# Value sums by thirds of a slab in one PSUM bank, and a ring of six PSUM banks numbered by a table

## The chip, the cores and the metric

One Trainium2 chip, one of its cores. The metric is the device time of one execution in microseconds (us). Engines are named PE (TensorE), DVE (VectorE), ACT (ScalarE), POOL (GpSimd) and SP (the queue that issues most transfers). The kernel is one launch of four blocks that run one after the other; all times below are of the whole launch.

## What is computed

The input is x, [4, 128, 96, 96]. The change touches only the second block, which works for this first half of the reference:

```python
kv = einsum('oc,bchw->bohw', qkv_w, gn(x))      # 1x1 convolution, 256 outputs
kv = dw3x3(kv, qkv_conv_w)                      # depthwise 3x3
k, v = split(kv, 2, axis=1)
q = ssl(gn(x), conv5_w, conv7_w, conv9_w)       # wavelet analysis, depthwise 3x3 per band, synthesis
# 8 heads of 16 channels: q and k normalised over the 9216 pixels
attn = softmax(einsum('bhdn,bhen->bhde', q, k) * temperature)
out = einsum('bhde,bhen->bhdn', attn, v)        # then a 1x1 projection, added to x
```

A second half (two binarised 3x3 convolutions with batch norm and a residual) follows; it is the fourth block.

## The kernel before

**The blocks.** `block_stats_and_projections` computes the group norm and the 1x1 projections and stores them (to about 190 us). `block_grams` (190 to 880 us) is the one the change touches. `block_attention` and `block_convolutions` follow.

**What `block_grams` does.** Its loop runs over NG = 32 slabs, numbered i = 0 to 31 here. One slab does two separate things. First, it handles 4 of the 128 channels, all four images, for keys and queries: separable filters as matrix products in split float16 (a high and a low part, three products for one), whose results go to `feat`; when four slabs (one head) are done, PE multiplies `feat` with itself into `gbank` (the gram) in pieces during the four slabs that follow. Second, it handles 12 rows of the values (SLAB = 12), all 128 channels: the depthwise 3x3 with nine taps. These value sums have nothing to do with the slab's filter jobs, but share the engines with them.

**Jobs.** A slab's filter work is 20 jobs, in the order of `SLOTS`, four rows of five: job 0 u, 1 kg, 2 mq, 3 s1, 4 tk; 5 kg, 6 s1, 7 mq, 8 u, 9 tk; 10 kg, 11 s1, 12 mq, 13 u, 14 tk; 15 kg, 16 s1, 17 mq, 18 u, 19 mq. Each job is summed by PE into one PSUM bank (L1059 to L1061 and L1069), then copied out as float16 by ACT (the high part, L965), then DVE subtracts that copy from the bank and so writes the low part (L1024). Here "low(n)" is the DVE step of job n. u and kg write `feat`, s1 writes `yh`/`yl`, mq writes `tmh`/`tml`, tk writes `tkh`/`tkl`. All three engines run the jobs in this order, with no reordering, and each waits by semaphores.

**What PE waits for.** Ahead of job n: that the bank is free, which is that low() of the bank's previous job is done (a ring of NB = 5 banks, so low(n-5)), and that its data are there. Job 0 (u) needs low(16) of the slab before, the s1 that wrote its operand; job 8 needs low(3), job 13 low(6), job 18 low(11). A DVE wait covers all earlier low() steps, since they run in order. After the last job of a row PE may run a piece of the gram of the head before (L1107, ten products).

**Value sums.** `seed` (L926, ACT) writes tap 0 of half a slab (6 rows of 96, 576 columns) into `vsum`, a PSUM tensor of two banks. `tap` (L1003, DVE) adds six more taps, each a scalar_tensor_tensor of 576 columns; the sixth writes to `vacc` in SBUF. Then the next half's seed may go. Each tap waits for the one before it. POOL adds taps 7 and 8 for the whole slab (`finish_slab`) after the last DVE tap. On DVE a tap runs right behind low(n) for each n in `TAP_AT`; on ACT a seed runs ahead of the copy of job n for each n in `SEED_AT`. `normalise` (four ACT instructions for the next slab's rows, L917) stands ahead of the copy of job 4, `high_x` ahead of that of job 13. In some slabs ACT also copies a finished gram (L944): ahead of job 11, right behind the copy of job 10, in the second slab that follows a head; right behind the copy of job 0 in the fourth.

**Kinds of slabs.** Slabs 0 to 3 have no gram beside them. From slab 4 on they repeat by four: kind 1 (i = 4, 8, ... 28) has gram pieces after jobs 9, 14 and 19; kind 2 after 4, 9 and 19, and the gram copy behind job 10; kind 3 after 4, 9, 14 and 19; kind 4 only a small product of edge terms after job 9, and the gram copy behind job 0. The slabs 4 to 27 are a hardware loop of three rounds of eight slabs; its two jumps back lie between slabs 11 and 12 and between 19 and 20. Slab 31 has no mq and tk jobs.

## Time and profile before

| | us |
|---|---|
| three timed runs | 1347.52, 1348.69, 1348.97 (median 1348.69) |
| the profiled execution, its own time | 1349.17 |
| its span, first to last instruction | 1347.2 |
| PE, DVE, ACT, POOL busy | 1158.6, 1009.5, 804.4, 533.7 |
| mean granted TensorE clock | 0.943 |

In the trace, DVE and ACT instructions overlap their neighbours: the next one starts some 0.08 us before the one ahead of it has ended. So what an instruction takes of its engine's time is the distance from its start to the next start, when nothing is waited for, and not its duration. A time in a "busy" column is a union of durations and hides short waits. PE's matmuls overlap in the same way.

### The profile page before, as it was taken

How to read it: one execution, taken by the hardware profiler on the slowest of the kernel's cores; microseconds unless marked ns; L12 is line 12 of the kernel's file. 1: busy time of each engine (PE TensorE's matmuls, PEld its weight loads, DVE VectorE, ACT ScalarE, POOL GpSimd, SP SyncE). 2: the span in 40 equal slices, each digit the busy share in tenths (PEclk: the TensorE clock that was granted, in tenths of full speed). 3: DMA queues.
4: the chain of work that ended last, by engine and by line, in shares of the span. 5: the costliest groups of instructions: out<-in, count | busy, mean ns of one | idle time of the engine just before them, and what ended most of it. 6: DMA issues, size and time to landing. Idle time of an engine off the chain costs nothing. (4 is left out here: it accounts for less than half of the span.)

```text
span 1347.2 us, 36311 instructions
## 1 busy us (share of the span) xinstructions
PE 1158.6 (86%) x12650; PEld 919.3 (68%) x12650; DVE 1009.5 (75%) x1802; ACT 804.4 (60%) x1414; POOL 533.7 (40%) x369
## 2 busy tenths in 40 slices
PE   0889978899999899998999999948999997999800
PEld 0445648889999899998999999825555554555500
DVE  6777557999999899998999999536767774153494
ACT  0567875777776677766777777212444446666292
POOL 6200023677686766867668776602000001000010
PEclk9999988999999899998999999878999998999955
DMA  9977793353553535535355354175778523000079
GB/s 320 417 245 304 304 301 78 94 150 101 126 151 98 131 103 129 147 102 133 98 133 145 101 138 114 41 264 196 265 244 279 190 82 123 1 0 0 1 312 406
DMA packets 148404, 221.24 MB, mean 164 GB/s; under 512 B 115202, under 2 KB 116492, under 8 KB 143896
## 3 DMA queue, kind: packets, MB, share of 16 engines
q1 hardware_dynamic: 136584, 152.18, 38.1%
q0 software_dynamic: 6480, 47.19, 9.2%
q10 hardware_dynamic: 5184, 19.76, 3.8%
q8 instruction: 101, 1.65, 0.6%
q14 instruction: 55, 0.45, 0.1%
HBM read 131.89 MB, written 87.20 MB: 163 GB/s over the span
## 5 line engine op out<-in xcount | busy, mean ns | idle before, releaser
L1746 PE MATMUL b_conv_bank<-b_sign,wsign 128*128 (+1 forms) x1728 | 299.9, 328 | 8.5 <-ACT b_sign L1544 7.5
L1017 DVE SCALAR_TENSOR_TENSOR b_value_sum<-b_vin,value_taps,b_value_sum 128x576 f32<-128x576 f32 x320 | 259.3, 810 | 16.3 <-ACT b_value_sum L934 15.5
L1746 PEld LDWEIGHTS b_conv_bank<-b_sign,wsign 128*128 128x128 bf16 x1728 | 168.1, 97 | 145.6 <-issue 31.7
L965 ACT CAST b_feat<-b_bank 96x400 f16<-96x400 f32 x255 | 125.7, 493 | 182.8 <-PE b_bank L1061 182.7
L1059 PE MATMUL b_bank<-b_tkh,b_kt 96*96 96x100 f16 x1536 | 224.3, 211 | 2.5 <-DVE b_tml L1040 2.2
L1060 PE MATMUL b_bank<-b_tkl,b_kt 96*96 96x100 f16 x1536 | 223.7, 211 | 0.0
L1061 PE MATMUL b_bank<-b_tkh,b_kt 96*96 96x100 f16 x1536 | 223.6, 211 | 0.0
L1059 PE MATMUL b_bank<-b_yh,b_tmh 96*96 96x200 f16 x768 | 195.1, 254 | 30.7 <-DVE b_feat L1024 14.4
L1059 PEld LDWEIGHTS b_bank<-b_tkh,b_kt 96*96 96x96 f16 x1536 | 195.2, 127 | 4.2 <-DVE b_tml L1040 2.5
L1061 PEld LDWEIGHTS b_bank<-b_tkh,b_kt 96*96 96x96 f16 x1536 | 195.3, 127 | 0.0
L1060 PEld LDWEIGHTS b_bank<-b_tkl,b_kt 96*96 96x96 f16 x1536 | 193.8, 126 | 0.0
L1061 PE MATMUL b_bank<-b_yh,b_tml 96*96 96x200 f16 x768 | 193.8, 252 | 0.0
L1060 PE MATMUL b_bank<-b_yl,b_tmh 96*96 96x200 f16 x768 | 193.6, 252 | 0.0
L812 POOL TENSOR_TENSOR b_vacc<-b_vacc,b_product 128x1152 f32<-128x1152 f32 x64 | 168.7, 2636 | 51.7 <-DVE b_vacc L1017 45.1
L1557 ACT CAST b_y<-b_conv_bank 128x384 f32 (+1 forms) x192 | 91.0, 475 | 126.5 <-PE b_conv_bank L1746 124.4
L1024 DVE TENSOR_TENSOR b_feat<-b_bank,b_feat 96x400 f16<-96x400 f32 x256 | 144.4, 564 | 25.9 <-ACT b_feat L965 21.1
L766 POOL TENSOR_TENSOR b_xl<-x_rows_store,b_xh 96x1536 f16<-96x1536 f32 x32 | 99.4, 3106 | 137.4 <-ACT b_xh L924 136.5
L1638 DVE BATCH_NORM_STATS2 b_bny<-b_y (+1 forms) x192 | 103.0, 553 | 58.3 <-ACT b_y L1557 57.8
L807 POOL TENSOR_TENSOR b_product<-b_vin,value_taps 128x1152 f32<-128x1152 f32 x64 | 134.8, 2106 | 6.0 <-POOL b_vacc L812 6.0
L1059 PEld LDWEIGHTS b_bank<-b_yh,b_tmh 96*96 96x96 f16 x768 | 95.1, 124 | 38.4 <-DVE b_feat L1024 18.6
L538 PE MATMUL b_pk<-b_x_first,b_w_image 128*128 128x384 f32 x288 | 102.2, 508 | 8.0 <-DVE b_khl L430 8.0
L965 ACT CAST b_tmh<-b_bank 96x504 f16<-96x504 f32 (+1 forms) x155 | 100.7, 650 | 0.0
(242 smaller groups left out, 2525.4 us busy)
## 6 DMA issues: line engine op xcount, KB each, us to landing
b_vin<-value_projection_scratch SPq DMA_DIRECT2D x32, 686.0 KB, 5.3
keys_scratch<-b_khl SPq DMA_DIRECT2D x24, 784.0 KB, 3.8
value_projection_scratch<-b_vout ACTq DMA_DIRECT2D x24, 784.0 KB, 4.7
b_kt<-keys_scratch SPq DMA_DIRECT2D x128, 147.0 KB, 3.3
x_rows_store<-in_x SPq DMA_DIRECT2D x128, 144.0 KB, 4.8
values_scratch<-b_vacc SPq DMA_DIRECT2D x32, 576.0 KB, 3.2
values<-values_scratch SPq DMA_DIRECT2D x48, 384.0 KB, 3.5
out<-xs SPq DMA_DIRECT2D x25, 576.0 KB, 6.9
```

Source lines behind the costliest of these rows:

```text
L538: nc.tensor.matmul(psum_k[g % NBK][:, 0:CH], w_image[:, b % 2, v, :], x[b][:, at:at + CH], start=True, stop=True).then_inc(s_mm, 1)
L766: nc.gpsimd.tensor_tensor(xh[1][:, slot, :, :, :].rearrange("h b c w -> h (b c w)"), xraw[:, slot, :], xh[0][:, slot, :, :, :].rearrange(" ...
L807: nc.gpsimd.tensor_tensor(vprod[:].rearrange("p (r c) -> p r c", c=W), vin[:, slot, :].rearrange("p (r c) -> p r c", c=WP)[:, t // 3:t // ...
L812: nc.gpsimd.tensor_tensor(vacc[:, slot, :], vacc[:, slot, :], vprod[:], ALU.add).then_inc(s_ptap, 1)
L965: nc.scalar.copy(*target(n, 0, k)).then_inc(s_hi, 1)
L1017: nc.vector.scalar_tensor_tensor(whole if t == DVE_TAPS[-1] else part, src, vtaps[:, t:t + 1], part, ALU.mult, ALU.add).then_inc(s_tap, 1)
L1024: nc.vector.tensor_tensor(out, src, high, ALU.subtract).then_inc(s_dve, 1)
L1059: nc.tensor.matmul(out, w_hi, m_hi, start=first, stop=False)
L1060: nc.tensor.matmul(out, w_hi, m_lo, start=False, stop=False)
L1061: return nc.tensor.matmul(out, w_lo, m_hi, start=False, stop=last)
L1638: V.bn_stats(bny[:, ds(r * RC + (b * NCH + k), 1), :].rearrange("p o s -> p (o s)"), y[:, b, ds(r * (RC * CH) + k * CH, CH)]).then_inc(s_b ...
L1746: ins = nc.tensor.matmul(cbank[k % NBK][:, 0:CH].rearrange("p (r c) -> p r c", c=W), p["wsign"][nth // NIMG][:, t * C:(t + 1) * C], padded ...
```

## The change

The value sums go by thirds of a slab in place of halves (PARTS = 3, PART = 4 rows, 384 columns), so `vsum` needs one PSUM bank in place of two. DVE issues 18 taps of 384 columns a slab in place of 12 of 576, ACT three seeds in place of two. The taps stand at new places, two of them behind low(4); the seeds stand ahead of jobs 1, 7 and 14 in place of 1 and 11. The bank that `vsum` gives up makes the ring of job banks six (NB = 6). Which job uses which bank is read from a table, `RING`: banks 0 and 1 are used every fifth job (0, 5, 10, 15 and 2, 7, 12, 17), the other four every sixth or seventh (1, 8, 14; 3, 9, 16; 4, 11, 18; 6, 13, 19). `last_use(n)` finds the job whose low() must be done. The eight builds ahead of the loop take their bank by their number modulo NB, as before. The rest is the same: the operations of the 20 jobs, their order, `NORMALISE`, `HIGH_X`, the gram pieces, POOL's work and all transfers.

```diff
@@ -576,12 +576,14 @@
         ana, map_place, map_diag, key_place, key_diag, null_cols = (
             p[n] for n in ("ana_parts", "map_place", "map_diag", "key_place", "key_diag", "null_cols"))
         PIECES = NIMG * H // STORE_ROWS // STORE_BUFS * 16
-        NB = 5
-        HALF = SLAB // 2
+        NB = 6
+        RING = (0, 2, 1, 3, 4, 0, 5, 1, 2, 3, 0, 4, 1, 5, 2, 0, 3, 1, 4, 5)
+        PARTS = 3
+        PART = SLAB // PARTS
         bank = [ctx.enter_context(nc.psum_tensor(f"b2_bank{i}", [C, 512], F32)) for i in range(NB)]
         gbank = ctx.enter_context(nc.psum_tensor("b2_gram", [C, 512], F32))
         last_gbank = [gbank, bank[0], bank[1]]
-        vsum = ctx.enter_context(nc.psum_tensor("b2_value_sum", [C, 2, 512], F32))
+        vsum = ctx.enter_context(nc.psum_tensor("b2_value_sum", [C, 512], F32))
 
         s_c = p["s_c"]
         s_z = sem("b2_pads_zeroed")
@@ -607,6 +609,11 @@
         s_gst = sem("b2_gram_stored")
         s_carry = sem("b2_wait_carrier")
 
+        def last_use(n):
+
+            return max(m for m in range(n) if RING[m] == RING[n]) if RING[n] in RING[:n] else max(
+                m for m in range(J) if RING[m] == RING[n]) - J
+
         NTK = -(-NKB // KPB)
         NTM = -(-NMB // MPB)
 
@@ -618,10 +625,10 @@
         )
         DVE_TAPS = (1, 2, 3, 4, 5, 6)
         POOL_TAPS = (7, 8)
-        NTAP = 2 * len(DVE_TAPS)
+        NTAP = PARTS * len(DVE_TAPS)
         PSTEPS = 2 * len(POOL_TAPS)
-        TAP_AT = (0, 2, 3, 5, 7, 8, 10, 12, 13, 15, 17, 18)
-        SEED_AT = (1, 11)
+        TAP_AT = (0, 1, 2, 3, 4, 4, 6, 7, 8, 9, 10, 11, 13, 14, 15, 16, 17, 18)
+        SEED_AT = (1, 7, 14)
         NORMALISE, HIGH_X = 4, 13
         LAG = {"s1": 0, "kg": 0, "u": 1}
         tk_jobs, mq_jobs = iter(range(NTK)), iter(range(NTM))
@@ -813,7 +820,7 @@
 
             def first_product(i, slot):
 
-                pool.wait_ge(s_seed, i * 2 + 1)
+                pool.wait_ge(s_seed, i * PARTS + 1)
                 pool.sem_inc(s_carry, 1)
                 product(slot, POOL_TAPS[0])
 
@@ -878,7 +885,7 @@
         def target(n, part, k):
 
             kind, c, old = jobs[n]
-            b = bank[n % NB]
+            b = bank[RING[n]]
             if kind == "s1":
                 return (ya[part][:, c % 2, :, 1:1 + SB], b[0:W, 0:NIMG * S2B].rearrange("p (n w) -> p n w", w=SB))
             if kind in builds:
@@ -923,16 +930,15 @@
                 act.wait_ge(s_xn, i + 1)
                 nc.scalar.copy(xh[0][:, slot, :, :, :].rearrange("h b c w -> h (b c w)"), xraw[:, slot, :]).then_inc(s_xh, 1)
 
-            def seed(k, i, half, loads):
+            def seed(k, i, part, loads):
 
                 slot = k % 2
-                if half == 0:
+                if part == 0:
                     act.wait_ge(s_vin[slot], loads * 16)
-                if half or not isinstance(i, int) or i:
-                    act.wait_ge(s_tap, i * NTAP + half * len(DVE_TAPS))
-                src = vin[:, slot, :].rearrange("p (r c) -> p r c", c=WP)[:, half * HALF:(half + 1) * HALF, 0:W]
-                nc.scalar.activation(vsum[:, :, 0:HALF // 2 * W].rearrange("p b (r c) -> p b r c", c=W),
-                                     src.rearrange("p (b r) c -> p b r c", b=2),
+                if part or not isinstance(i, int) or i:
+                    act.wait_ge(s_tap, i * NTAP + part * len(DVE_TAPS))
+                nc.scalar.activation(vsum[:, 0:PART * W].rearrange("p (r c) -> p r c", c=W),
+                                     vin[:, slot, :].rearrange("p (r c) -> p r c", c=WP)[:, part * PART:(part + 1) * PART, 0:W],
                                      ACT.Copy, scale=vtaps[:, 0:1]).then_inc(s_seed, 1)
 
             def copy_gram(head, e, gbank=gbank):
@@ -1002,19 +1008,18 @@
 
             def tap(k, i, m, loads):
 
-                slot, half, t = k % 2, m // len(DVE_TAPS), DVE_TAPS[m % len(DVE_TAPS)]
-                src = vin[:, slot, :].rearrange("p (r c) -> p r c", c=WP)[:, half * HALF + t // 3:(half + 1) * HALF + t // 3,
+                slot, part, t = k % 2, m // len(DVE_TAPS), DVE_TAPS[m % len(DVE_TAPS)]
+                src = vin[:, slot, :].rearrange("p (r c) -> p r c", c=WP)[:, part * PART + t // 3:(part + 1) * PART + t // 3,
                                                                           t % 3:t % 3 + W]
-                src = src.rearrange("p (b r) c -> p b r c", b=2)
-                whole = vacc[:, slot, half * HALF * W:(half + 1) * HALF * W].rearrange("p (b r c) -> p b r c", b=2, c=W)
-                part = vsum[:, :, 0:HALF // 2 * W].rearrange("p b (r c) -> p b r c", c=W)
+                done = vacc[:, slot, part * PART * W:(part + 1) * PART * W].rearrange("p (r c) -> p r c", c=W)
+                total = vsum[:, 0:PART * W].rearrange("p (r c) -> p r c", c=W)
                 if t == DVE_TAPS[0]:
-                    dve.wait_ge(s_seed, i * 2 + (half + 1))
+                    dve.wait_ge(s_seed, i * PARTS + (part + 1))
                 else:
                     dve.wait_ge(s_tap, i * NTAP + m)
                 if m == len(DVE_TAPS) - 1:
                     dve.wait_ge(s_vst[slot], loads * 16)
-                nc.vector.scalar_tensor_tensor(whole if t == DVE_TAPS[-1] else part, src, vtaps[:, t:t + 1], part,
+                nc.vector.scalar_tensor_tensor(done if t == DVE_TAPS[-1] else total, src, vtaps[:, t:t + 1], total,
                                                ALU.mult, ALU.add).then_inc(s_tap, 1)
 
             def low(n, k):
@@ -1029,7 +1034,7 @@
                     if active(n, how):
                         dve.wait_ge(s_hi, i * J + (count(n, how) + LEAD))
                         low(n, k)
-                    if n in TAP_AT:
+                    for _ in range(TAP_AT.count(n)):
                         tap(k, i, m, pairs + (k // 2 + 1))
                         m += 1
                 assert m == NTAP, m
@@ -1072,7 +1077,7 @@
 
             def run(n, k):
                 kind, c, old = jobs[n]
-                b = bank[n % NB]
+                b = bank[RING[n]]
                 slot = (k - old) % 2
                 ring = c % 2
                 if kind == "s1":
@@ -1136,9 +1141,9 @@
 
                 for n, (kind, c, old) in enumerate(jobs):
                     if active(n, how):
-                        m = n - NB if n >= NB else max(m for m in range(J) if m % NB == n % NB) - J
+                        m = last_use(n)
                         while m >= 0 and not active(m, how):
-                            m = m - NB if m >= NB else max(q for q in range(J) if q % NB == n % NB) - J
+                            m = last_use(m)
                         need(m)
                         if kind == "s1" and c == 0:
                             pe.wait_ge(s_xl, i + 1)
@@ -1153,7 +1158,7 @@
                         if kind in builds:
                             if c == 0:
                                 pe.wait_ge(s_rk if kind == "tk" else s_rm, i + 2)
-                            build(kind, c, bank[n % NB], (k + 1) % 2)
+                            build(kind, c, bank[RING[n]], (k + 1) % 2)
                         else:
                             run(n, k)
                     if gram is not None and n in row_end:
```

## Rows read from the trace of the kernel before

**Rows 1.** The page, span in 40 slices of 33.7 us, digits are tenths.

```profile
DVE  6777557999999899998999999536767774153494
PEclk9999988999999899998999999878999998999955
```

**Rows 2.** By slab: busy PE, PEld, DVE, ACT, POOL; clock, DMA share, GB/s.

```profile
261.80:281.40 19.60, 17.56 (x286) 16.64 (x286) 19.02 (x34) 14.24 (x29) 13.43 (x8) 1.00 0.52 119
531.50:551.10 19.60, 18.85 (x305) 18.43 (x306) 19.03 (x34) 14.09 (x27) 16.66 (x17) 1.00 0.36 104
551.10:572.20 21.10, 20.56 (x324) 20.01 (x323) 19.34 (x33) 15.43 (x29) 16.07 (x9) 1.00 0.65 147
572.20:592.10 19.90, 19.90 (x317) 19.45 (x316) 19.07 (x33) 14.10 (x27) 13.61 (x8) 1.00 0.46 117
592.10:612.90 20.80, 19.95 (x337) 19.00 (x335) 19.08 (x33) 15.32 (x30) 13.22 (x8) 1.00 0.54 138
612.90:638.30 25.40, 22.25 (x301) 22.04 (x302) 19.31 (x34) 14.20 (x27) 19.27 (x18) 0.80 0.35 97
```

**Rows 3.** Groups of instructions, 200 to 880 us: busy, mean ns, idle before, releasers.

```profile
L1059 PE MATMUL b_bank<-b_yh,b_tmh 96*96 96x200 f16 x768 | 195.1, 254 | 30.7 <-DVE b_feat L1024 14.4 <-DVE b_yl L1024 8.2 <-DVE b_tml L1024 4.1
```

**Rows 4.** Timeline of DVE, slab 3: start, duration, instruction, [idle before].

```profile
261.79 0.57 DVE L1024 TENSOR_TENSOR b_yl<-b_bank,b_yh 96x400 f16<-96x400 f32 x1
...
270.20 0.64 DVE L1024 TENSOR_TENSOR b_tkl<-b_bank,b_tkh 96x468 f16<-96x468 f32 x1 [0.58 <-ACT b_tkh L965]
...
276.01 0.81 DVE L1017 SCALAR_TENSOR_TENSOR b_value_sum<-b_vin,value_taps,b_value_sum 128x576 f32<-128x576 f32 x1
276.73 0.57 DVE L1024 TENSOR_TENSOR b_yl<-b_bank,b_yh 96x400 f16<-96x400 f32 x1
...
281.39 0.57 DVE L1024 TENSOR_TENSOR b_yl<-b_bank,b_yh 96x400 f16<-96x400 f32 x1
```

**Rows 5.** Timeline of PE at the start of slab 3.

```profile
262.50 0.26 PE L1059 MATMUL b_bank<-b_yh,b_tmh 96*96 96x200 f16 x1 [0.98 <-DVE b_yl L1024]
```

**Rows 6.** Timeline of ACT, slab 3, jobs 0 to 4.

```profile
264.97 0.74 ACT L934 ACTIVATE b_value_sum<-b_vin,value_taps 128x576 f32<-128x576 f32 x1 [0.20 <-DVE b_vacc L1017]
265.91 0.49 ACT L965 CAST b_feat<-b_bank 96x400 f16<-96x400 f32 x1 [0.20 <-PE b_bank L1061]
...
267.23 2.50 ACT L917 ACTIVATE x_rows_store<-x_rows_store,row_stats 96x384 f32<-96x384 f32 x4
269.63 0.54 ACT L965 CAST b_tkh<-b_bank 96x468 f16<-96x468 f32 x1
```

**Rows 7.** Timeline of DVE in the first block: 384 columns, and two dependent steps.

```profile
90.95 0.60 DVE L430 SCALAR_TENSOR_TENSOR b_khl<-b_pk,b_bias,b_khl 128x384 f16<-128x384 f32 x1
91.47 1.27 DVE L334 BATCH_NORM_STATS2 b_bn<-b_x_first 128x6 f32<-128x512 f32 x2
...
113.45 0.22 DVE L395 SCALAR_TENSOR_TENSOR b_col<-b_col 128x1 f32<-128x1 f32 x1
113.71 0.15 DVE L396 TENSOR_SCALAR b_col<-b_col 128x1 f32<-128x1 f32 x1
```

**Rows 8.** Timeline of DVE, kind 2 (551.1 to 572.2).

```profile
560.01 0.65 DVE L1024 TENSOR_TENSOR b_tkl<-b_bank,b_tkh 96x468 f16<-96x468 f32 x1 [0.59 <-ACT b_tkh L965]
...
566.68 0.82 DVE L1017 SCALAR_TENSOR_TENSOR b_value_sum<-b_vin,value_taps,b_value_sum 128x576 f32<-128x576 f32 x1 [0.79 <-ACT b_value_sum L934]
```

**Rows 9.** Timeline of ACT, kind 2, gram copy and second seed.

```profile
565.04 1.06 ACT L944 COPY b_gout<-b_gram 128x512 f32<-128x512 f32 x1
565.90 0.75 ACT L934 ACTIVATE b_value_sum<-b_vin,value_taps 128x576 f32<-128x576 f32 x1
```

**Rows 10.** Timeline of DVE, kind 4 (592.1 to 612.9).

```profile
597.59 0.82 DVE L1017 SCALAR_TENSOR_TENSOR b_value_sum<-b_vin,value_taps,b_value_sum 128x576 f32<-128x576 f32 x1 [0.95 <-ACT b_value_sum L934]
...
601.75 0.64 DVE L1024 TENSOR_TENSOR b_tkl<-b_bank,b_tkh 96x468 f16<-96x468 f32 x1 [0.35 <-ACT b_tkh L965]
```

**Rows 11.** Timeline of PE at the jump back ahead of slab 20.

```profile
616.05 0.39 PE L1059 MATMUL b_bank<-b_yh,b_tmh 96*96 96x200 f16 x1 [3.39 <-DVE b_feat L1024]
```

## The prediction

> **What bounds the kernel now.** The page's chain of work that ended last reaches back only to 916 us, behind the block in question, so it doesn't say what sets the pace there. The page's slices come first: in the slices of `block_grams` both PE and DVE stand at 9 tenths, and TensorE's clock is at its upper level but for three dips [rows 1]. So the table of busy time slab by slab is the view to read [rows 2]. It shows that the pace isn't one number. A slab without gram takes 19.6 us with PE busy 17.6 and DVE 19.0. In kind 3 PE is busy for all 19.9 us: there PE is the bound. Kind 2 takes 21.1 though DVE is busy 19.3, kind 4 takes 20.8. DVE does the same work in each slab, so its 19.0 says how near it stands to being the bound in all of them.
>
> Then the timeline of DVE in slab 3. From low(16) of the slab before (261.79) to the same step one slab on (281.39) are 19.60 us, with a single wait of note: 0.58 ahead of low(4) [rows 4]. I cut the slab there. The **front**, low(16) to low(4), is 270.20 - 261.79 = 8.41 us; the **rest**, low(4) to the next low(16), is 281.39 - 270.20 = 11.19 us, in which DVE never stands still: it is a sum of DVE's starts. The front is a chain over three engines: low(16) ends at 262.36, PE starts job 0 at 262.50 after an idle time that ended with it [rows 5], jobs 0 and 1 run, ACT copies job 1 at 265.91, then jobs 2 and 3, then `normalise` from 267.23, then job 4 at 269.63 [rows 6], and low(4) starts at 270.20 [rows 4].
>
> **What the change does to DVE's time.** A tap of 576 columns takes 276.73 - 276.01 = 0.72 us from start to next start [rows 4]. The trace has the same operation with PSUM input at 384 columns, in the first block: 91.47 - 90.95 = 0.52 us [rows 7]. Both fit 0.12 us plus a column each 1.04 ns, so the 0.12 is paid per instruction. Per slab the taps go from 12 x 0.72 = 8.64 us to 18 x 0.52 = 9.36 us. Two taps behind low(4) have nothing between them and the second waits for the first: start to start is then the duration plus about 0.04 us (0.22 and 0.26 in the two dependent steps, [rows 7]), 0.60 + 0.04 = 0.64 in place of 0.52, so 0.12 more. DVE's bill is 0.72 + 0.12 = 0.84 us a slab. The price of a tap is bounded below by 0.48 us (0.72 x 384 / 576, no price per instruction) and above by its duration of 0.60 us [rows 7]; I take 0.52, the row with the same operation, columns and kind of source.
>
> The Trainium skill, VectorE: DVE Perf Modes, section The TRN2 errata, speaks against the change: many small tiles pay a fixed latency each, so tile to 512 elements or more. By its formula for back-to-back fp32 work, (N + 151) / 0.96 ns, the smaller size costs 6 x 151 / 0.96 = 0.94 us a slab, an estimate, against the 0.72 that the rows give; the sum below would be some 7 us higher.
>
> **Where the new time lies.** In the front, DVE had 5 taps (behind 17, 18, 0, 2, 3) and gets 7 (16, 17, 18, 0 to 3): 5 x 0.72 = 3.60 against 7 x 0.52 = 3.64 us, and the 0.58 of idle time covers it. The chain there doesn't change: job 0 needs low(16) as data, which no bank changes, and `normalise` stays ahead of job 4. In the rest, 7 taps (behind 5, 7, 8, 10, 12, 13, 15) become 11: 7 x 0.72 = 5.04 against 11 x 0.52 + 0.12 = 5.84, so 11.19 becomes 11.99 us. Nothing covers that, if PE and ACT deliver in time.
>
> I walked the new order by these durations, low(16) at 0. low(4) 8.41, the two taps 8.97 and 9.61, low(5) 10.13. Seed 2 goes when the tap ends (10.2) and takes between 0.49 (two thirds of today's 0.74, [rows 6]) and 0.74 us; I take 0.59, near the middle, and even 0.74 has it done at 10.95, where the next tap wants it at 11.1. Job 10 (kg) needs low(5) in both kernels, bank 0 being used every fifth job; low(5) is now 1.1 us later, so PE idles until 10.75, but it still delivers job 10 to ACT at 12.6, and low(10) comes only at 14.8. Job 15 starts at 15.4 and is copied by 18.3, low(15) is due at 19.3. low(16) comes at 20.35. So DVE keeps full and **a slab without gram takes 20.4 us in place of 19.6**. I add 0.05 for the third hand-over of a seed.
>
> **What the sixth bank gives.** PE's waits for feat's low() ahead of u jobs (14.4 us, [rows 3]) are mostly those for the bank, at jobs 13 and 18; they go. But in a slab whose pace is DVE's, PE only waits at another job: job 10 and job 0. The gain is where PE was late. By kind, the same walk:
> - Kind 1 (19.54 before): front as before, rest +0.80, PE's gram pieces fall into its new gaps: **+0.86**.
> - Kind 2 (21.14: front 8.94, from 551.07 to 560.01 [rows 2, 8], and rest 12.20): the rest holds a stall of 0.79 [rows 8], because the gram copy of 1.06 us stands ahead of the second seed on ACT [rows 9], and some 0.2 behind it. The seeds now stand ahead of 7 and 14, neither behind the copy: 11.99. The front is long today because PE comes late to job 0, still at its gram piece; with DVE 0.8 later in kind 1, PE is less late and the front is 8.5. Sum 20.5: **-0.64**.
> - Kind 3 (19.93): PE-bound 19.9 [rows 2]; DVE now wants 20.4, above PE's sum: **+0.47**.
> - Kind 4 (20.80): its front of 9.61 has the gram copy and then the seed ahead of job 1, a stall of 0.95 on DVE [rows 10]. The copy stays there, the seed is 0.15 shorter and PE comes 0.3 earlier: 9.14. Rest +0.80: **+0.32**.
>
> **The sum.** Slabs 0 to 3: 4 x 0.85 = +3.4. Kind 1, seven: +6.0, less 0.4 at each of the two jumps back, where PE arrives that much earlier at a stall of 3.4 us [rows 11] that itself stays: -0.8. Kind 2, seven: -4.5. Kind 3, seven: +3.3. Kind 4 without slab 31, six: +1.9. Slab 31, all taps but fewer low() steps, so that six more pairs of taps are adjacent: its last low() 0.5 later: +0.5. Together +9.8 us on the profiled execution's own 1349.17 (which lies 0.5 above the median of 1348.69): **1359.0 us**. POOL, SP and transfers keep their order: the last DVE tap stays behind low(18). The block behind starts later by as much.
>
> **Rivals.**
> - *A tap's price goes by columns alone* (0.48 us, the lower bound). For it: the first operation at 384 columns writes float16 to SBUF, not PSUM, and today's tap spans two banks. Against it: the fixed 0.12 is the same at both sizes. Each slab is then 11 x 0.04 = 0.44 cheaper: 1359.0 - 32 x 0.44 = 1345 us, faster than before.
> - *Bubbles on PE are the bound and the sixth bank removes them.* All 14.4 us of bank waits go and DVE's bill hides: 1349.2 - 14.4 = 1335 us. Against it: DVE idles 0.58 us in slab 3 [rows 4], less than its bill. The Trainium skill, Trainium Kernel Development and Optimization, section Best Practices, says that consistent bubbles can mean that PSUM ran out; by that rule this case would be the outcome. The same bubbles are also what a ring looks like that waits for DVE.
> - *The bill hides and nothing is gained*: DVE's idle share in kinds 2 and 4 takes it, 1349 us. It needs every front to shorten, and only two can.
> - *Nothing comes back in kinds 2 to 4*: new waits behind seeds eat the gains, and all 32 slabs pay 0.8: 1349.2 + 26 = 1375 us. Speaks for it: low(7) has only 0.1 us to spare behind seed 2.
> - *The clock falls.* PE's idle now comes in two stretches of 1.5 us a slab (ahead of jobs 10 and 0). Waits of 1 us leave the clock at 2.4 GHz [rows 5, 2]; the one of 3.4 brings it to 1.2 GHz, mean 0.80 in that slab, and the slab takes 25.4 in place of 19.5 [rows 2, 11], of which 3.1 is the stall itself and 2.7 the slow clock. From a point between 1 and 3.4 us it decides; ten slabs (0 to 3 and some of kind 1) would give 1359 + 27 = 1386 us.
>
> **Chances.** Forecast 0.65 (1353 to 1366); columns alone 0.11; bubbles 0.04; hides 0.07; nothing comes back 0.08; the clock 0.05. What a measurement can tell from no change is about 0.2%, 2.7 us. Faster 0.15, same 0.09, slower 0.76. The range runs from 1347, which takes in half of the faster case's spread, to 1373: the error of 0.02 us in a tap's price alone is 18 x 0.02 x 25 DVE-bound slabs = 9 us.
>
> **What the profile after would show.** Right: 576 taps of 384 columns, 0.52 us from start to start and 0.64 for the pair behind low(4); slabs of 20.4 without gram; DVE without a wait from low(4) to low(16) in all kinds; ACT's normalise still ahead of DVE's one idle stretch; PE's idle time ahead of job 10 on feat's low(5). Wrong: taps of 0.48; waits of DVE on seeds; slabs of 19.6; more stretches at 1.2 GHz.

## The result and the profile after

| | before | after |
|---|---|---|
| median of 8 runs each, us | 1348.24 (1346.06 to 1352.02) | 1354.55 (1352.98 to 1358.85) |
| the profiled execution, its own time and span | 1349.17, 1347.2 | 1354.76, 1353.1 |
| DVE, ACT busy, us | 1009.5, 804.4 | 1028.0, 815.0 |
| mean granted TensorE clock | 0.943 | 0.945 |

The changed kernel is slower: ratio 1.0055, 95% interval 1.0039 to 1.007. The forecast was 1359.0.

The page of after, the slices that answer to [rows 1], and two of its costliest groups (instruction, count, busy us, mean ns, idle time before it and what ended that):

```profile
DVE  6767557999999899998999999636767764153494
...
PEclk9999988999999899999999999877999998999955
...
L1022 DVE SCALAR_TENSOR_TENSOR b_value_sum<-b_vin,value_taps,b_value_sum 128x384 f32<-128x384 f32 x480 | 294.4, 613 | 8.7 <-ACT b_value_sum L940 8.5
L1064 PE MATMUL b_bank<-b_yh,b_tmh 96*96 96x200 f16 x768 | 195.0, 254 | 24.3 <-DVE b_yl L1029 10.7
```

The taps are at 384 columns (480 here, and 96 that write `vacc`), and PE's idle time ahead of u jobs fell from 30.7 us [rows 3] to 24.3. Ahead of the kg jobs it rose from 0.2 to 14.5, all of it a wait for DVE. From 200 to 880 us, before and then after:

```profile
L1059 PE MATMUL b_bank<-b_tkh,b_kt 96*96 96x100 f16 x1525 | 221.5, 211 | 0.2
L1064 PE MATMUL b_bank<-b_tkh,b_kt 96*96 96x100 f16 x1524 | 221.0, 211 | 14.5 <-DVE b_feat L1029 14.5
```

So PE stands still in these two groups for 38.8 us in place of 30.9, with one bank more.

The windows by slab, from low(16) to low(16), answer to [rows 2]: slab 3, then slabs 16 to 20, which are kinds 1, 2, 3, 4 and the slab behind the second jump back (slab 20, itself of kind 1). Columns as there (length, busy PE, PEld, DVE, ACT, POOL, granted clock, DMA share, GB/s).

```profile
263.55:283.91 20.36, 17.25 (x286) 16.63 (x286) 19.77 (x39) 14.64 (x29) 13.44 (x8) 1.00 0.50 130
535.09:555.49 20.40, 19.36 (x309) 18.72 (x310) 19.71 (x40) 14.24 (x28) 15.82 (x17) 1.00 0.37 107
555.49:575.96 20.47, 20.47 (x323) 19.97 (x321) 19.75 (x39) 15.84 (x31) 15.74 (x9) 1.00 0.56 144
575.96:596.36 20.40, 20.27 (x320) 19.65 (x319) 19.71 (x40) 14.14 (x27) 14.28 (x8) 1.00 0.47 124
596.36:617.29 20.93, 19.38 (x332) 18.53 (x329) 19.75 (x39) 16.09 (x32) 13.77 (x8) 1.00 0.52 133
617.29:640.97 23.68, 20.94 (x309) 20.32 (x310) 19.86 (x40) 14.13 (x28) 19.07 (x18) 0.93 0.40 111
```

The slabs have become nearly equal, 20.4 us, with DVE busy 19.7 of them; kind 4 keeps half a microsecond above that. The last row is the surprise: 25.4 before, 23.68 now.

The timeline of DVE in slab 3, against [rows 4] (start, duration, instruction, idle time before it):

```profile
263.55 0.58 DVE L1029 TENSOR_TENSOR b_yl<-b_bank,b_yh 96x400 f16<-96x400 f32 x1
...
271.98 0.64 DVE L1029 TENSOR_TENSOR b_tkl<-b_bank,b_tkh 96x468 f16<-96x468 f32 x1 [0.56 <-ACT b_tkh L971]
272.54 0.61 DVE L1022 SCALAR_TENSOR_TENSOR b_value_sum<-b_vin,value_taps,b_value_sum 128x384 f32<-128x384 f32 x1
273.18 0.62 DVE L1022 SCALAR_TENSOR_TENSOR b_vacc<-b_vin,value_taps,b_value_sum 128x384 f32<-128x384 f32 x1
273.71 0.56 DVE L1029 TENSOR_TENSOR b_feat<-b_bank,b_feat 96x400 f16<-96x400 f32 x1
...
278.88 0.61 DVE L1022 SCALAR_TENSOR_TENSOR b_value_sum<-b_vin,value_taps,b_value_sum 128x384 f32<-128x384 f32 x1
279.39 0.57 DVE L1029 TENSOR_TENSOR b_yl<-b_bank,b_yh 96x400 f16<-96x400 f32 x1
...
283.91 0.58 DVE L1029 TENSOR_TENSOR b_yl<-b_bank,b_yh 96x400 f16<-96x400 f32 x1
```

A tap takes 279.39 - 278.88 = 0.51 to 0.52 us from start to start, the first of the adjacent pair 273.18 - 272.54 = 0.64. The front is 8.43 us (8.41 before), with the same idle time ahead of low(4); the rest is 11.93 (11.19 before) without a wait.

PE in the same slab, its two waits of over 1 us:

```profile
264.28 0.26 PE L1064 MATMUL b_bank<-b_yh,b_tmh 96*96 96x200 f16 x1 [1.31 <-DVE b_yl L1029]
274.33 0.24 PE L1064 MATMUL b_bank<-b_tkh,b_kt 96*96 96x100 f16 x1 [1.41 <-DVE b_feat L1029]
```

They stand ahead of job 0 and of job 10, as forecast. The waits for the bank at jobs 13 and 18 (0.41 and 0.47 us in slab 3 before) have gone, and PE now waits that much and more at these two places, with 0.38 ahead of job 15.

### The profile page after: what moved, and what is told of

Its sections match the earlier page's. It is cut to its first block and busy times, and to the rows that moved or that the text cites. A ratio compares the mean times of both kernels' runs of the same rounds, so it can differ in the third digit from the quotient of the medians.

```text
span 1353.1 us, 36508 instructions
## 1 busy us (share of the span) xinstructions
PE 1158.7 (86%) x12650; PEld 918.0 (68%) x12650; DVE 1028.0 (76%) x1994; ACT 815.0 (60%) x1446; POOL 533.8 (39%) x369
## 5 line engine op out<-in xcount | busy, mean ns | idle before, releaser
L1022 DVE SCALAR_TENSOR_TENSOR b_value_sum<-b_vin,value_taps,b_value_sum 128x384 f32<-128x384 f32 x480 | 294.4, 613 | 8.7 <-ACT b_value_sum L940 8.5
L1064 PE MATMUL b_bank<-b_tkh,b_kt 96*96 96x100 f16 x1536 | 224.1, 211 | 17.2 <-DVE b_feat L1029 14.5
L1064 PE MATMUL b_bank<-b_yh,b_tmh 96*96 96x200 f16 x768 | 195.0, 254 | 24.3 <-DVE b_yl L1029 10.7
L1064 PEld LDWEIGHTS b_bank<-b_tkh,b_kt 96*96 96x96 f16 x1536 | 194.4, 127 | 23.8 <-DVE b_feat L1029 19.5
L1029 DVE TENSOR_TENSOR b_tml<-b_bank,b_tmh 96x504 f16<-96x504 f32 (+1 forms) x155 | 100.4, 648 | 0.0
```

What stands on the lines that cost most here:

```text
L1022: nc.vector.scalar_tensor_tensor(done if t == DVE_TAPS[-1] else total, src, vtaps[:, t:t + 1], total, ALU.mult, ALU.add).then_inc(s_tap, 1)
L1029: nc.vector.tensor_tensor(out, src, high, ALU.subtract).then_inc(s_dve, 1)
L1064: nc.tensor.matmul(out, w_hi, m_hi, start=first, stop=False)
```

## The experiments

Times are medians; each ratio is against the kernel before on the same chip, with its 95% interval. Slab times are read from low(16) to low(16) as above.

**How far the slabs repeat.** A second profile of each of the two kernels (1348.54 and 1354.79 us) gives slabs 1 to 31 within 0.03 us of the first, but for the two behind a jump back and slab 21 of the kernel before (21.44 us, again 21.54). Behind the jumps, before takes 25.42 and 25.35 us, again 24.96 and 25.53; after 24.96 and 23.68, again 23.84 and 24.98. Differences of 0.1 us in a kind can be read from one profile, a single jump can't; the two jumps together differ between the kernels by 2.1 us in the first pair of profiles and by 1.7 in the second.

**Is it the thirds, and what is the sixth bank worth?** `e1_thirds_five_banks` keeps the thirds and gives the bank back:

```diff
-        NB = 6
-        RING = (0, 2, 1, 3, 4, 0, 5, 1, 2, 3, 0, 4, 1, 5, 2, 0, 3, 1, 4, 5)
+        NB = 5
+        RING = (0, 1, 2, 3, 4) * 4
```

> The changed kernel with the ring back at five banks, every bank used each fifth job; thirds, taps and seeds stay. My theory: slabs without gram run at DVE's sum from low(4) to low(16), the banks set only where PE waits, and what kinds 2 to 4 gained came from the seeds' new places and from DVE being later, not from the bank. Then slabs stay at 20.35, 20.4, 20.5, 20.4 and 20.9 us and the time within 1.5 us of the changed kernel's 1354.6. Rival, the sixth bank pays: kind 2 goes back to 21.1 and kind 4 up by 0.3, some 6 us in all, 1360.

Measured: 1357.6 us, ratio 1.0066 (1.0048 to 1.0083). All kinds are within 0.03 us of after but for kind 2, 20.69 instead of 20.47. So the thirds, with their new places for taps and seeds, carry the whole loss and most of the gain in kind 2, and the sixth bank is worth 0.2 us in each of seven slabs, 1.5 us. The ratios, each against the kernel before timed beside it, say the same: 1.0066 against 1.0055, 1.5 us. The medians of e1 and after are 3.0 us apart; the kernel before was itself 1.1 us slower beside e1, and the two slabs behind a jump (25.50 and 24.13 us), which vary by as much, took 1.0 more. What the bank is worth in the kernels with thirds below, where PE waits elsewhere, wasn't run.

**Does moving a tap, with no work added or taken away, take the loss back?** `e2_pair_in_front` moves one of the two taps from behind low(4) to behind low(3), from the rest into the front:

```diff
-        TAP_AT = (0, 1, 2, 3, 4, 4, 6, 7, 8, 9, 10, 11, 13, 14, 15, 16, 17, 18)
+        TAP_AT = (0, 1, 2, 3, 3, 4, 6, 7, 8, 9, 10, 11, 13, 14, 15, 16, 17, 18)
```

> The changed kernel with one of the two taps behind low(4) moved behind low(3), so that the pair that waits for itself stands there and eight taps lie in the front, ten in the rest. My theory: the front's idle time of 0.56 us covers the moved tap (front 8.4 to 8.5), the rest loses 0.64 us and goes to 11.3. Slab without gram 19.8 in place of 20.35; kind 1 19.8, kind 2 20.0, kind 3 20.4 (PE-bound), kind 4 20.4: 13 us less than the changed kernel, 1341 to 1343, under the kernel before. Rival: PE or the chain over ACT bounds, the place of a tap is worth nothing, 1354.

Measured: 1340.42 us, ratio 0.9934 (0.9911 to 0.9957). Slabs without gram 19.72, kinds 1 to 4 19.65, 20.37, 19.73, 21.09. DVE and windows of this kernel, slab 3, and the slab behind the first jump:

```profile
272.45 1.27 DVE L1022 SCALAR_TENSOR_TENSOR b_value_sum<-b_vin,value_taps,b_value_sum 128x384 f32<-128x384 f32 x2
273.62 0.64 DVE L1029 TENSOR_TENSOR b_tkl<-b_bank,b_tkh 96x468 f16<-96x468 f32 x1
```

```profile
265.20:284.92 19.72, 17.25 (x286) 16.64 (x286) 19.68 (x40) 14.62 (x29) 13.44 (x8) 1.00 0.53 127
446.60:468.67 22.07, 19.60 (x308) 18.86 (x309) 19.68 (x40) 14.09 (x28) 17.51 (x17) 1.00 0.43 120
```

The idle time ahead of low(4) is filled by the pair. DVE's sum, 19.72 us, is now the length of a slab without gram; that is the floor of the thirds as they are ordered. Moved work was worth more than the removed waits of PE. The total is in part luck. The expectation was 20.0, 20.4 and 20.4 us for kinds 2, 3 and 4, and only the misses' opposite signs bring the sum near it: in kind 4 a feat copy and a seed still make DVE wait 0.50 and 0.79 us, and the tap that was moved has nothing to fill. And by the profiles 3.4 us of the gain on after lie at the jumps, where the clock did not fall at all in e2 (see below); the other slabs from 1 to 30 give 11.4.

**Did ACT's `normalise` set the front?** `e5_normalise_at_5` moves it behind the copy of job 4, `e4_normalise_at_9` ahead of the copy of job 9:

```diff
-        NORMALISE, HIGH_X = 4, 13
+        NORMALISE, HIGH_X = 5, 13
```

> The changed kernel with ACT's four normalise instructions ahead of the copy of job 5, so behind that of job 4 and ahead of the second seed. In the run with them at job 9 the front fell to DVE's own sum (7.77 us), but they then stood behind the seed that waits for the sixth tap, and the copy of job 9 came 0.88 us late. At 5 they end 1.3 us before that seed is due. My theory: front 7.8, rest 11.95, slab without gram 19.75, kind 1 19.8, kind 2 20.1, kind 3 20.3 (PE), kind 4 20.5: 1341 to 1343. Rival: the normalise only moves its price from one wait to the next, 1352 or more.

> The changed kernel with ACT's four normalise instructions ahead of the copy of job 9 in place of job 4. My theory: they are what low(4) waits for at the end of the front; without them DVE runs from low(16) to low(4) at its own sum, 7.8 to 7.9 us in place of 8.4. Slab without gram 19.9, kind 1 19.9, kind 2 20.0, kind 3 20.4 (PE-bound), kind 4 20.5: 11 to 12 us less than the changed kernel, about 1343. Rival: the front is set by job 0 waiting for low(16), then 1354.

Measured: at 5 1342.9 us, ratio 0.9944 (0.9923 to 0.9965); at 9 1365.3, ratio 1.0123 (1.0107 to 1.014). ACT and DVE with `normalise` at 5:

```profile
266.25 0.58 ACT L971 CAST b_tkh<-b_bank 96x468 f16<-96x468 f32 x1
266.70 2.51 ACT L924 ACTIVATE x_rows_store<-x_rows_store,row_stats 96x384 f32<-96x384 f32 x4
```

```profile
260.82 0.57 DVE L1029 TENSOR_TENSOR b_yl<-b_bank,b_yh 96x400 f16<-96x400 f32 x1
...
268.60 0.64 DVE L1029 TENSOR_TENSOR b_tkl<-b_bank,b_tkh 96x468 f16<-96x468 f32 x1
```

The front is 7.78 us, all of it DVE's own work, and the slab 19.72: the 2.5 us of `normalise` ahead of job 4 did set it. Kind 4 stayed at 21.07 us where 20.5 had been expected, for the same two waits as in e2 (0.48 and 0.79). The two slabs behind a jump took 24.74 and 24.46 us, and each of the slabs behind them, 13 and 21, 21.24 in place of the 20.27 of its kind, PE being busy throughout. With `normalise` at 9 the front is as short (7.77), and the gain is lost further on:

```profile
273.30 0.58 ACT L940 ACTIVATE b_value_sum<-b_vin,value_taps 128x384 f32<-128x384 f32 x1 [1.87 <-DVE b_vacc L1022]
273.82 0.67 ACT L971 CAST b_tmh<-b_bank 96x504 f16<-96x504 f32 x1
274.37 0.48 ACT L971 CAST b_feat<-b_bank 96x400 f16<-96x400 f32 x1
274.75 2.51 ACT L924 ACTIVATE x_rows_store<-x_rows_store,row_stats 96x384 f32<-96x384 f32 x4
277.15 0.57 ACT L971 CAST b_tkh<-b_bank 96x468 f16<-96x468 f32 x1
```

ACT has 1.87 us of nothing to do, but it spends them in the wait of the second seed for the sixth tap, ahead of `normalise`. Copy 9 comes late, low(9) waits 0.88 us for it, and the slab takes 20.68:

```profile
277.75 0.64 DVE L1029 TENSOR_TENSOR b_tkl<-b_bank,b_tkh 96x468 f16<-96x468 f32 x1 [0.88 <-ACT b_tkh L971]
```

I had taken ACT's idle time as free at any place of its queue; in an engine that works in order it is free only where the idle time itself stands.

**Is kind 2's gain a gain of the thirds?** `e3_copies_moved` is the kernel before with only ACT's gram copies at other places, so that no seed stands right behind one:

```diff
-        START, COPY_AT, NULL_AT = [0, 6], [5, 11, 14], 12
+        START, COPY_AT, NULL_AT = [0, 6], [(1, 15), (3, 5), (3, 15)], 12
...
-                    if gram is not None and n - 1 in [-1] + row_end and chunk(k, n) in COPY_AT:
-                        copy_gram(gram, COPY_AT.index(chunk(k, n)))
+                    if gram is not None and (k % GPH, n) in COPY_AT:
+                        copy_gram(gram, COPY_AT.index((k % GPH, n)))
```

> The kernel before with ACT's gram copies moved: the first from behind job 10 to behind job 15 of kind 2, the second from behind job 0 to behind job 5 of kind 4. Halves, five banks, taps and seeds as before. My theory: the stalls of 0.79 and 0.95 us ahead of a tap go; kind 2 comes from 21.1 to about 20.2, kind 3 stays PE-bound and takes part of it back, kind 4 loses 0.3: about 1 us a head, 1340 to 1342 against 1348.2. It shows that kind 2's gain in the changed kernel is no merit of thirds or banks. Rival: PE bounds these slabs, nothing moves, 1348.

Measured: 1340.94 us, ratio 0.993 (0.9908 to 0.9952), kinds 1 to 4 at 19.54, 20.29, 20.05, 20.52.

```profile
301.06:321.35 20.29, 20.29 (x323) 19.94 (x322) 19.32 (x33) 15.33 (x29) 16.18 (x9) 1.00 0.44 113
```

Kind 2 is at PE's own sum (busy 20.29 of 20.29) with halves and five banks. So the better order of seed and gram copy, which needs neither thirds nor a bank, gives more in kind 2 (21.13 to 20.29) than the whole change does (to 20.48). In the changed kernel 0.2 of the 0.65 us is the sixth bank, by e1; that the rest is this order fits the wait of 0.79 us that has gone [rows 8, 9], and wasn't run by itself with thirds.

**Do the two cures add up?** `e7_pair_front_and_copies` is the changed kernel with the edits of e2 and e3. `e6_halves_split_normalise` is e3 with `normalise` cut up, images 0 and 1 ahead of job 4, image 2 ahead of 5, image 3 ahead of 6. `e8_halves_copy_behind_8` is e6 with the second gram copy behind job 8 instead of 5, that is (3, 8) for (3, 5).

```diff
-        NORMALISE, HIGH_X = 4, 13
+        NORMALISE, HIGH_X = {4: (0, 1), 5: (2,), 6: (3,)}, 13
```

> The changed kernel (thirds, six banks) with both cheap moves: one of the paired taps from behind low(4) to behind low(3), and the gram copies behind job 15 of kind 2 and job 5 of kind 4. My theory: kind 4, 21.1 us in the run with the pair alone because of the copy and the seed ahead of job 1, comes to 19.8 to 20.1; slab without gram stays 19.7, kind 1 19.7, kind 2 20.0, kind 3 20.3: 79.9 a head against 80.8, so 6 us under that run, 1334 to 1336. Rival: kind 4 only pays what kind 3's late PE leaves, 1340.

> The kernel before (halves, five banks, twelve taps) with the gram copies moved as in the run of that change, and normalise in pieces: two images ahead of the copy of job 4, one ahead of 5, one ahead of 6. My theory: DVE's twelve large taps are the cheaper bill (18.97 us a slab against 19.7), and with nothing late on ACT the slabs come to 19.05 without gram, 19.2, 19.9, 20.6, 19.5 by kind: some 14 us under the kernel before, 1334, under every variant with thirds. Rival: with five banks PE waits for banks as soon as DVE is full, no better than the run with the copies alone, 1341.

> The kernel before with halves, five banks, normalise in pieces as in the run with split normalise, and the second gram copy behind job 8 of kind 4 in place of 5. My theory: the 0.45 us that low(6) waited in kind 4 goes, 20.5 becomes 20.0 there: 3 us less, 1337.5. Rival: the copy's 0.85 us lands on the copy of job 9 or on the seed ahead of 11, no change, 1340.8.

Measured: e7 1340.6 us, ratio 0.9952 (0.9936 to 0.9968); e6 1340.81, ratio 0.9927 (0.9903 to 0.9951); e8 1351.84, ratio 1.0018 (0.9999 to 1.0037). None of them passes e2 and e3, and all three theories missed; e7 and e6 came out at their rivals' times. In e7 kind 2 fell to 19.96, as hoped, kind 3 took 19.90, and kind 4 stayed at 21.05, where 19.8 to 20.1 had been expected: 80.5 us a head in place of 79.9:

```profile
585.52:606.57 21.05, 19.97 (x339) 19.18 (x337) 19.95 (x40) 16.23 (x33) 14.08 (x8) 1.00 0.53 137
```

Kinds 2 and 3 are now PE's (busy 19.96 of 19.96, and 19.90 of 19.90), and in kind 4 DVE waits 0.50 and 0.52 us for feat copies; that PE enters kind 4 late, as the rival had it, fits this and wasn't tested apart. In e6 slabs without gram fell to 18.93 us and kind 1 to 18.87, but kinds 2 and 3 are PE's (busy for all of 20.66 and 20.05) and kind 4 stayed at 20.48. Kind 2 took back 0.37 of the 0.67 us that kind 1 gave: what one kind gives, the next takes, as PE's work is not spread evenly over them. One of its slabs shows more:

```profile
241.39:260.32 18.93, 17.16 (x286) 16.62 (x286) 18.93 (x34) 14.24 (x28) 13.46 (x8) 1.00 0.43 116
260.32:282.16 21.84, 20.35 (x286) 19.81 (x286) 19.22 (x34) 14.30 (x28) 13.41 (x8) 0.84 0.51 127
```

The same work twice, and in the second slab the clock is at its lower level (1.2 GHz) for 6.8 us from 261.0 on, though PE's longest wait around it is 0.98 us and in the first of the two rows, with the clock up throughout, PE did the same. It happened once in this execution, cost that slab 2.9 us, and its trigger stays open. In e8 the product of edge terms (L1122) waits for the gram copy, which now lies behind the copies of jobs 7 and 8; PE and the window of that slab:

```profile
520.33 0.96 PE L1122 MATMUL b_gram<-b_edge 96*16 96x16 f32 x32 [1.84 <-ACT b_gout L946]
```

```profile
508.35:532.10 23.75, 21.91 (x331) 21.59 (x329) 19.46 (x34) 15.27 (x29) 14.10 (x8) 0.86 0.40 107
```

1.84 us of waiting, and the clock falls at 521.3 for 6.8 us. Four slabs on, the same wait (1.85 us) leaves it up:

```profile
591.67:613.11 21.44, 19.44 (x337) 18.94 (x334) 19.38 (x33) 15.34 (x30) 13.20 (x8) 1.00 0.47 123
```

All six slabs of kind 4 with a whole job list have this wait, 1.84 to 1.86 us. In three of them the clock falls for 6.8 us and the slab takes 23.3 to 23.8, in one for 3.4 (22.18), in two not at all (21.44), against 20.48 in e6. So the copy costs 1 us a slab by the wait and up to 2.3 more by the clock. I had priced the copy by DVE's and ACT's queues and not by its reader on PE.

**The jumps back.** They were the largest miss of the prediction, so the last two runs take them away: `e9_halves_unrolled` is the kernel before, `e10_thirds_unrolled` the changed one, each with the 24 looped slabs written out.

```diff
-            with pe.Fori(0, LOOPS) as hh:
+            for hh in range(LOOPS):
```

and the same on SP, POOL, ACT and DVE, the rest unchanged.

> The kernel before with the 24 slabs of its hardware loop written out (no jump back on any engine), all else the same. Theory (the two slabs behind a jump take 25.4 us in place of 19.5 only because of the jump: PE's wait of 3.4 to 4.1 us and the slow clock that follows it): slabs 12 and 20 take 19.55 us like every kind 1, the clock stays at its upper level from 228 us to the end of the block, and the time falls by 5.87 + 5.80 = 11.7 us (less 0.3 more in slab 21), to 1349 - 12 = 1337 us (1335 to 1339). Rival (the wait is the fetch of instructions as such, and code that is written out pays it elsewhere, a little in every slab): slabs 12 and 20 come down but others rise, 1343 to 1350 us, with more idle time of the engines that nothing of the kernel releases.

> The changed kernel with its 24 looped slabs written out, all else the same. Theory (by the slabs the change costs some 10 us, and 2 to 3 of them came back at the two jumps only because PE's wait there is shorter and the clock falls for less time): slabs 12 and 20 take 20.4 us like every kind 1, the time falls by only 4.55 + 3.27 = 7.8 us, to 1354.6 - 7.8 = 1347 us (1345 to 1349), so 9 to 10 us above the kernel before with the same loop written out, where the two kernels with loops differ by 6. The end of the block still has the clock at its lower level for some 10 us, 3 longer than in the kernel before. Rival (the gain at the jumps is one of execution to execution, and the two kernels differ by the same 6 us without jumps): 1343 us.

Measured: e9 1340.37 us, ratio 0.9928 (0.9909 to 0.9947); e10 1346.01, ratio 0.9982 (0.9964 to 1.0). PE at job 0 of slab 12, where the jump was, in before, after, e9 and e10, one fence each:

```profile
448.05 0.40 PE L1059 MATMUL b_bank<-b_yh,b_tmh 96*96 96x200 f16 x1 [4.09 <-DVE b_tml L1024]
```

```profile
450.81 0.40 PE L1064 MATMUL b_bank<-b_yh,b_tmh 96*96 96x200 f16 x1 [3.07 <-DVE b_tml L1029]
```

```profile
442.56 0.26 PE L1059 MATMUL b_bank<-b_yh,b_tmh 96*96 96x200 f16 x1 [0.98 <-DVE b_yl L1024]
```

```profile
447.78 0.26 PE L1064 MATMUL b_bank<-b_yh,b_tmh 96*96 96x200 f16 x1 [1.31 <-DVE b_yl L1029]
```

And the windows of slab 12 in e9, then e10:

```profile
441.85:461.46 19.61, 18.80 (x305) 18.41 (x306) 19.03 (x34) 14.07 (x27) 16.93 (x17) 1.00 0.41 115
```

```profile
447.07:467.44 20.37, 19.34 (x309) 18.74 (x310) 19.78 (x40) 14.25 (x28) 16.02 (x17) 1.00 0.41 115
```

Without the jump both kernels start job 0 0.71 us after low(16), the clock stays at 2.4 GHz through the whole stretch from 226 to 848 us, and slabs 12 and 20 cost what every kind 1 costs. So the 5.4 to 6.0 us that a jump costs the kernel before are the jump's alone. The DVE step that the two rows with a jump name as the releaser isn't what job 0 needs: that is low(16), which ended 3.25 us ahead of it in the kernel before.

The DMA records of the traces show what arrives in between. The page of the profile lists a queue q8 of kind instruction; its loads are of 16 KiB. In all 24 jumps of the twelve profiles with a loop, the last of these loads ahead of job 0 starts 2.6 to 3.4 us ahead of it: with halves from 0.04 us ahead of low(16) to 0.93 behind it, with thirds from 1.10 us ahead of it to level with it. In e9 and e10 none starts in the 5 us ahead of job 0 of these slabs. The Trainium skill, Runtime: NRT & Kernel Launch, section Instruction fetch mechanics, says that a taken branch breaks the sequential fetch of instructions, and that one whose target isn't at hand stalls until the target has been fetched. The trace agrees, with these loads and with waits of 2.34 to 4.09 us; that job 0 waits for the load is argued from the times, as no view names it as the releaser.

From low(16) of slab 0 to low(16) of slab 30 the two kernels with loops differ by 629.86 - 626.40 = 3.5 us, the two without by 621.91 - 614.75 = 7.2. So the change costs its slabs 7.2 us, and 3.7 of that came back at the jumps, somewhat more than the theory's 2 to 3. The totals didn't follow it. e10 is within its range, but e9, expected at 1335 to 1339, lies between its theory and its rival, so that the two differ by 1346.0 - 1340.4 = 5.6 us where 9 to 10 had been expected and 6 was the rival's. Behind low(16) of slab 30 e9 takes 509.8 us, the kernel before 504.6: 1.6 of the 5.2 are at the end of the block, with the clock down for 10.2 us instead of 6.8, the other 3.6 in what follows. In e10 the same stretch is 507.5 to after's 506.9. The stretch behind the block varies by itself: it took 2.0 us more in the second profile of after than in the first. So whether the halves lose there because they are written out isn't settled.

## Why the prediction held, and where it didn't

The predicted and the measured difference of the two profiled executions, by the prediction's own terms (us):

| term | predicted | measured |
|---|---|---|
| slabs 0 to 3 | +3.4 | +3.2 |
| kind 1, five away from the jumps | +4.3 | +4.2 |
| the two slabs behind a jump | +0.9 | -2.1 |
| kind 2, seven | -4.5 | -4.9 |
| kind 3, seven | +3.3 | +3.1 |
| kind 4, six | +1.9 | +0.8 |
| end of the block | +0.5 | +2.2 |
| first block, and what follows | 0 | -0.5 |
| sum of the span (the measured terms add to 6.0 by rounding) | +9.8 | +5.9 |

**A tap's price.** 0.52 us from start to start was right, from the one row at 384 columns; the rival by columns alone (0.48) is out. The pair cost the 0.12 more that two dependent steps had shown. By the Trainium skill's formula (VectorE: DVE Perf Modes, section The TRN2 errata) the prediction's estimate had a slab 0.22 us longer than by the rows. The Trainium skill states it of an fp32 `tensor_tensor` add, not for this operation nor from start to start; slabs 2 and 3 grew by 0.76, so the measurement decides for the rows.

**Front and rest.** Front 8.43 for 8.41, rest 11.93 for 11.99. e5 shows the cause that the prediction named for the front: with `normalise` behind job 4 it falls to DVE's own 7.78. e2 shows what bounds the rest, DVE's work in it, as 0.64 us of that moved forward made the slab 0.64 shorter. Kind 2 came out as it was added up, 8.54 for 8.5 and 11.94 for 11.99.

**The sixth bank.** As forecast, PE's waits moved to jobs 10 and 0 and gained little where DVE sets the pace; e1 puts the bank at 1.5 us. The rival in which bubbles are the bound is out.

**The kinds.** Kinds 1, 2 and 3 were right within 0.1 us each. For kind 4 the mis-sized step is the front: 605.36 - 596.36 = 9.00 us where 9.14 was predicted ("the seed is 0.15 shorter and PE comes 0.3 earlier"). A wait of 0.42 us for a feat copy that before had there has gone, and the wait for the seed is 0.71 for 0.95. The rest is 11.94 for 11.99.

```profile
605.36 0.64 DVE L1029 TENSOR_TENSOR b_tkl<-b_bank,b_tkh 96x468 f16<-96x468 f32 x1 [0.43 <-ACT b_tkh L971]
```

It is 0.2 us a slab, 1.1 in all.

**The jumps.** The step that failed is "at a stall of 3.4 us that itself stays". It didn't stay: PE waits 3.07 and 2.90 us where it waited 4.09 and 3.39, in the second profiles 3.04 and 2.85 for 3.40 and 3.37. PE's earlier arrival is there as forecast, 0.3 us for 0.4 (its last product ends 0.59 us ahead of low(16), before 0.27), and it comes on top. Above what their kind takes, the two jumps cost 11.7 us in before and 7.9 in after (11.4 and 8.0 in the second profiles). Of these 3.9 us less (3.4), 2.2 (1.6) are job 0's earlier start after low(16), and the other 1.7 (1.8) the slow clock, which was priced as fixed: behind the two jumps it stood at 1.2 GHz for 17.1 us in both profiles of before, for 10.2 in both of after. The term is off by 3.0 us, of a total error of 3.9.

The clock's part doesn't follow from the shorter wait. e5 has thirds and waits of 3.10 and 2.89 us, as after has, but the clock was down for 10.2 us behind each, and its two jumps cost 11.6 us, as much as those of before; e2, with waits of 2.34 and 2.41, had no slow stretch. That the wait is the jump's is shown by e9 and e10. Why it is shorter with the thirds isn't; the instruction load ahead of job 0 starts earlier there. The wait for the bank ahead of job 18 (0.38 us in before, none in after) isn't the reason: e3 and e8, with halves, have no such wait in the slab ahead of a jump, and PE waits 3.19 to 3.83 us at their jumps.

The prediction also split a jump's price wrongly, into a stall of 3.1 and 2.7 us of slow clock. Job 0 starts 3.1 us after low(16) there, but 0.7 us after it in a slab without a jump, so the stall adds 2.4 and the slow clock 3.4, which is also PE's extra busy time (22.25 for 18.85 [rows 2]). It changes only the clock rival, ten slabs of 3.4 in place of 2.7.

**The end of the block.** The step "its last low() 0.5 later" was mis-sized. DVE's last tap comes 0.65 us later against low(16) of slab 30, but low(18) behind it 1.6 us later, 1.3 in the second profiles, because it also waits for PE. The windows from 20 us behind that low(16) on, before and then after:

```profile
862.59:882.00 19.41, 16.22 (x150) 13.37 (x148) 1.05 (x2) 2.79 (x4) 13.22 (x13) 0.82 0.14 43
```

```profile
866.16:887.80 21.64, 17.85 (x150) 14.82 (x150) 1.49 (x3) 2.79 (x4) 13.20 (x13) 0.76 0.13 40
```

The same 150 products take 1.6 us more of PE, at a mean clock of 0.76 for 0.82. PE waits 2.37 us ahead of the last u job, before 1.53, and the clock was down for 10.2 us in place of 6.8. The longer stretch isn't a price of the change: in the second profile of after it was 6.8 us behind the same wait of 2.37, and the next block began only 0.6 us later than in before, not 2.2; and e9 had 10.2 behind the 1.53 of before. That second execution of after was no shorter, as what follows the block took 2.0 us more.

The misses have both signs, -3.0 and -1.1 against +1.7, and the last is one execution's: that the total is off by 3.9 and not by more is in part luck. The median of after is 4.5 us under the forecast, well inside the range. The clock rival didn't happen: PE's waits of 1.3 and 1.4 us in slabs 2 and 3, and one of 1.2 to 1.3 in each kind 1, left the clock up, in e10 from 226 to 857 us.

## What to carry to other kernels

Price a split of work by start-to-start rows at the new size, then ask for each stretch of the slab which engine is full in it: a resource that removes the waits of an engine that isn't the bound moves these waits, and no more. Before buying PSUM space with extra instructions, look at the order on the engine that copies: here one long ACT step ahead of a needed copy was worth 12 us (after to e5, by the medians; 15 by the ratios, 11.9 in the slabs away from the jumps), and a seed behind a gram copy 7 to 9 us with halves and five banks (before to e3). In a queue that works in order, idle time is free only where it stands, as e4 paid for, and a step that is moved has a price at each engine that waits for it, as e8 paid for.

## What the runs showed of the hardware that I had not expected

A hardware loop's jump back cost 5.4 to 6.0 us a time in the kernel before, and 3.3 to 4.6 in the changed one: a PE wait of 2.9 to 4.1 us and 3.4 to 10.2 us at half clock around it or behind it. Written out, the same 24 slabs cost none of it. In the DMA records a load of 16 KiB of instructions starts 2.6 to 3.4 us ahead of the first product behind each jump; the row's releaser names a DVE step instead.

The clock's answer to a wait isn't a fixed price. Waits of 2.34 and 2.41 us at the jumps (e2) left it at 2.4 GHz, six waits of 1.84 to 1.86 us in another place (e8) were followed by 6.8 us at 1.2 GHz three times, by 3.4 once and by none twice, and in e6 it fell once as a wait of 0.98 ended. Waits of 2.9 us at a jump had 3.4 us of slow clock in after and 10.2 in e5. A forecast that counts a stall has to leave some 3 us open for the clock behind it.
